# Moving a softmax's normalisation from the probabilities to the attention output

## Chip, cores and metric

One core of a Trainium2 chip runs the whole kernel. The metric is the device time of one execution, in microseconds.

## What is computed

Two sequences of 1024 tokens, 128 features, go through half a feed-forward layer (attention and experts), a sparse attention, and half a feed-forward layer again. The change lies in the sparse attention. Cut to what matters (B = 2 sequences; the program cuts 1024 tokens into tiles of 128; 8 heads):

```
x = x + 0.5 * ffn(layernorm(x))
x = x + attn(layernorm(x))
x = x + 0.5 * ffn(layernorm(x))

def attn(x):                                   # for every token t and head h
    c_kv = x @ W_dkv                           # 32 latent features per token
    I    = index scores of t against all earlier tokens
    idx  = top_k(I with the last 64 tokens set to +inf, 96)   # 64 local keys + 32 selected
    scores = (q_c . key_c[idx] + q_r . key_r[idx]) * scale
    attn   = softmax(scores)                   # over the 96 keys
    out    = sum_k attn[k] * value[idx[k]]     # value = c_kv @ W_uv
    return out @ W_out
```

W_uk, W_uv and W_out are folded by the kernel into two small matrices, so that keys and values of a token are both 32 latent features (plus 32 + 32 for the rotated part of the key).

## The kernel before

The attention runs over NB = 128 blocks of 16 tokens. A block has 16 x 8 = 128 rows (token, head), so scores and probabilities fill the 128 partitions; their 256 columns are 128 local positions and 4 x 32 selected ones. Blocks come in pairs, far, near, far, near (`place`). A far block lies in the second half of its sequence: its selected rows are fetched by POOL, four indirect DMAs (L620), into one of six buffers G. A near block lies in the first half: POOL makes one-hot matrices from the index list (L639, one to four per block), and PE multiplies the tables TAB by them (L1001). Sixteen blocks are a phase; there are 8. The selection for phase q (top 32 by `max`, `max_index`, `match_replace`, `dve_select`) runs on DVE in the steps of the phase before. The last piece of it, the near list, is made in iteration 16q - 3 of the loop (L1662 or L1664); SP stores it to DRAM and reads it back to all partitions (L501, L507); then POOL can make the phase's one-hots. The far list goes by PE and ACT (L1242) to POOL. 

A row of keys and values has ROWG = 128 columns: 64 of the rotated key, 32 latent (DC), and 32 that hold 1.0 (L598, `KVS[:, :, ROWKV:]`). Before the change the loop reads the first ROWKV = 96 only.

Every engine works in the order of its program, iteration i = 0 to 127:

- PE: `pe_turned(i)` (transposes the probabilities PB into bank 6, L1029; for near blocks the values too, L1032), `pe_keys(i+3)` (L995, L1001), `pe_scored(i+2)` (L1014, L1017, mask L1020), index scores L982 where due, `pe_mixed(i)` (values times probabilities into bank 7, L1045, L1048).
- DVE: `dve_inverse(i+1)` (L1697), `dve_keys(i+3)` (L1683, multiplies the keys by the rotation), `dve_least(i+2)` (L1692, the row minimum, since scores are held negated), every fourth iteration `dve_attended` (L1707, copies four blocks of bank 7 to OA), and the selection steps.
- ACT: `act_turned(i)` (L1271, bank 6 to PTS), the queries L1261, `act_scaled(i+1)` (L1284, multiplies the probabilities by 1/sum), `act_exp(i+2)` (L1278, exp with the row sum in `total` by `accum_out`), index scores L1249, L1252.
- SP moves OA to OAX (L515, 16 transfers a phase) after `oa_ready`; PE's last product (L951) needs all of them.

So the probabilities are normalised before they are transposed: exp and its sum on ACT, the reciprocal of one column on DVE, the scaling on ACT (`pn_ready`), then PE. Bank 7 holds four groups of 4 blocks, 32 partitions each.

Of the kernel before, what the change touches and what calls it, by code (L numbers as in the profile page):

```python
# [12 lines left out]
ALU = mybir.AluOpType  # L13
# [3 lines left out]
P = 128  # L17
# [179 lines left out]
def build(nc, ins, const_ap, rot_ap, mask_ap, out):  # L197
# [9 lines left out]
    with ExitStack() as ctx:  # L207
# [55 lines left out]
        total = sb("total", [P, 3])  # L263
        inverse = sb("inverse", [P, 3])
# [62 lines left out]
        KV64 = view("sel", (NT, DC))  # L327
# [24 lines left out]
        PTS = [ATTf[:, i * 3 * P:(i + 1) * 3 * P] for i in range(2)]  # L352
        PB = [ATTf[:, 6 * P + i * 2 * P:6 * P + (i + 1) * 2 * P] for i in range(3)]
# [53 lines left out]
        inverse_ready, pn_ready = sem("inverse_ready"), sem("pn_ready")  # L407
# [109 lines left out]
        def sp_sel(sp):  # L517
# [14 lines left out]
            for b in range(B):  # L532
                t = b * TB
                sp.dma_start(KV64[0:LW, t + 1:t + TB, :], KVS[LW:P, t:t + TB - 1, 2 * DR:ROWKV]).then_inc(kv64_loaded, 16)
                sp.dma_start(KV64[LW:P, t:t + TB, :], KVS[0:LW, t:t + TB, 2 * DR:ROWKV]).then_inc(kv64_loaded, 16)
                sp.dma_start(KV64[0:LW, t, :], KVS[0:LW, t, 2 * DR:ROWKV]).then_inc(kv64_loaded, 16)
# [448 lines left out]
        def pe_keys(pe, x):  # L985
# [5 lines left out]
            if far:  # L991
                d = 8 * q + k
                pe.wait_ge(gathered[d % GR], 16 * GB * (d // GR + 1))
                for g in range(GB):
                    m = pe.transpose(o[0:ROWKV, g * P:(g + 1) * P], G[d % GR][:, g, 0:ROWKV], ident)  # L995
            else:
                b, n = tile // TB, chunks(tile, k)
                for c in range(n):
                    pe.wait_ge(oh_ready, OH_AT[x][c] + 1)
                    for part in range(2):  # L1000
                        m = pe.matmul(o[0:ROWKV, :], TAB[part][:, 4 * b + c, 0:ROWKV], OH[OH_AT[x][c] % OHR][:, :],  # L1001
                                      start=(c == 0 and part == 0), stop=(c == n - 1 and part == 1))
# [19 lines left out]
        def pe_turned(pe, x):  # L1022

            q, far, tile, k = place(x)
            pe.wait_ge(pn_ready, x + 1)
            if x >= 1:
                pe.wait_ge(pts_ready, x)
            for part in range(2):
                m = pe.transpose(bank[6][:, part * P:(part + 1) * P], PB[x % 3][:, part * P:(part + 1) * P], ident)  # L1029
            if not far:  # L1030
                for g in range(GB):
                    m = pe.transpose(bank[6][:, 2 * P + g * DC:2 * P + (g + 1) * DC],  # L1032
                                     GTS[x % 3][2 * DR:ROWKV, g * P:(g + 1) * P], ident[2 * DR:ROWKV, 2 * DR:ROWKV])
            m.then_inc(tp_done, 1)

        def pe_mixed(pe, x):
# [4 lines left out]
            if slot == 0 and j >= 4:  # L1041
                pe.wait_ge(oa_ready, j - 3)
            o = bank[7][j % 4 * DC:(j % 4 + 1) * DC, slot * P:(slot + 1) * P]
            pts = PTS[x % 2]
            pe.matmul(o, KVS[:, tile, 2 * DR:ROWKV] if k >= 4 else KV64[:, tile, :], pts[:, 0:P], start=True, stop=True)  # L1045
# [756 lines left out]
```

## Time and profile before

| | |
|---|---|
| median of 3 runs | 2058.41 us (2049.06 to 2064.82) |
| the profiled execution | 2058.41 us |
| its span | 2056.6 us |
| attention loop (first L1278 to last L1707) | about 792 to 1432 us |
| busy in the whole span | PE 84%, DVE 63%, ACT 54%, POOL 27% |

A row of "lines" or of the page gives line, engine, operation, tiles (written <- read), shapes and count, then busy time and mean ns, then the engine's idle time before them and what ended it. A row of the order of time gives start, duration, engine and line; in brackets stands how long the engine was idle before it and which instruction ended that. PEld is the loading of weights, beside PE.

### The profile page before, as it was taken

Reading aid. Unit: us, or ns where it says so; the run is one execution under the profiler, and the core shown is the slowest. Engines: PE = TensorE matmul, PEld = TensorE weight load, DVE = VectorE, ACT = ScalarE, POOL = GpSimd, SP = SyncE. Lnnn points to the kernel's source line nnn. Section 1 sums busy time; section 2 is a strip of 40 time slices with the busy share of each in tenths; the row PEclk is TensorE's granted clock in tenths of the full one; section 3 lists DMA queues with packets and bytes.
Section 4 is the critical chain, followed back from the end, with each engine's and each line's share of the span. In section 5 each row is a group of like instructions: output and inputs, shape, how many; then the busy total and the mean of one; then the engine's idle time right before and its main releaser. Section 6 shows DMA issues by size and latency. Waiting matters only on the chain.

```text
span 2056.6 us, 33763 instructions
## 1 busy us (share of the span) xinstructions
PE 1720.3 (84%) x10588; PEld 999.4 (49%) x10588; DVE 1287.6 (63%) x3053; ACT 1111.6 (54%) x2328; POOL 548.3 (27%) x479
## 2 busy tenths in 40 slices
PE   3799999699967357888987978989489999969995
PEld 1344444477754114454654545556234444447774
DVE  5677775577785665464555645533467777557777
ACT  3367777388845343434344334323237767738883
POOL 6000000000001504786656867662500000000000
PEclk9699999699987566777567768567769999969998
DMA  4111110012102142101021111120211111002110
GB/s 132 64 49 50 48 46 9 27 66 83 51 2 88 62 110 49 42 28 50 28 63 46 29 46 31 43 64 18 92 62 49 50 50 44 9 30 85 61 52 21
DMA packets 66504, 104.26 MB, mean 51 GB/s; under 512 B 19432, under 2 KB 37296, under 8 KB 63280
## 3 DMA queue, kind: packets, MB, share of 16 engines
q1 hardware_dynamic: 56720, 84.86, 12.8%
q0 software_dynamic: 8192, 16.79, 2.8%
q8 instruction: 72, 1.18, 0.2%
q10 hardware_dynamic: 1456, 0.90, 0.2%
q14 instruction: 64, 0.52, 0.1%
HBM read 74.80 MB, written 8.59 MB: 41 GB/s over the span
## 4 chain that ended last, share of the span: by engine, by line
PE 58%; POOL 13%; issue 10%; DVE 8%; ACT 4%; SPq 3%; DVEq 2%; DMA 1%; ACTq 0%; another core or an unknown queue 0%; POOLq 0%
PE bank L701 10%; PE bank L847 8%; PE bank L685 7%; POOL onehot L639 7%; POOL arena L620 6%; PE bank L660 6%; PE bank L837 6%; PE bank L1001 2%; PE bank L1014 2%; ACT experts L1146 1%; PE bank L662 1%; PE bank L687 1%; PE bank L1029 1%; DVE arena L1313 1%; PE bank L1017 1%
## 5 line engine op out<-in xcount | busy, mean ns | idle before, releaser
L1313 DVE TENSOR_REDUCE arena<-bank 128x1 f32<-128x512 f32 (+3 forms) x768 | 382.9, 551 | 170.1 <-PE bank L662 117.3
L1073 ACT ACTIVATE arena<-bank 128x512 f32<-128x512 f32 (+3 forms) x768 | 335.2, 493 | 144.3 <-PE bank L687 121.5
L566 POOL TENSOR_TENSOR rstd<-vareps,neghalf 128x8 f32<-128x8 f32 x14 | 23.8, 1698 | 1168.0 <-DVE vareps L1306 1168.0
L660 PE MATMUL bank<-arena 72*128 72x512 bf16 (+3 forms) x768 | 259.8, 346 | 39.1 <-DMA arena<-arena 37.0
L620 POOL DMA_INDIRECT arena<-kv_rows,IDX x256 | 250.8, 980 | 155.9 <-ACT IDX L1242 86.7
L685 PE MATMUL bank<-arena 99*128 99x512 bf16 (+3 forms) x768 | 254.4, 335 | 6.0 <-ACT arena L1079 4.3
L639 POOL TENSOR_SCALAR onehot<-XT,const 128x512 fp32r<-128x512 f16 x136 | 212.4, 1573 | 160.7 <-DMA XT<-idx_rows 76.7
L701 PE MATMUL bank<-arena 128*32 128x512 f32 (+3 forms) x1536 | 225.4, 501 | 0.0
L1683 DVE TENSOR_TENSOR HN<-bank,RT 96x512 f32<-96x512 f32 x128 | 87.3, 682 | 206.8 <-PE bank L1001 144.2
L1371 DVE TENSOR_TENSOR experts<-arena,experts 128x512 fp32r<-128x512 f32 x256 | 171.6, 689 | 71.1 <-ACT experts L1146 71.1
L1144 ACT ACTIVATE arena<-bank,bias 128x512 f32<-128x512 f32 x256 | 185.6, 725 | 46.1 <-PE bank L837 46.0
L1278 ACT ACTIVATE ATT<-bank,col 128x256 f32<-128x256 f32 x128 | 60.6, 473 | 272.1 <-DVE col L1692 242.1
L837 PE MATMUL bank<-experts,experts 128*128 128x512 f32 x768 | 196.6, 403 | 7.5 <-ACT experts L1146 5.5
L1146 ACT ACTIVATE experts<-bank,bias 128x512 fp32r<-128x512 f32 x256 | 186.9, 730 | 0.0
L1001 PE MATMUL bank<-onehot,tab 128*96 128x512 f32 x272 | 123.8, 576 | 72.2 <-POOL onehot L639 72.2
L847 PE MATMUL bank<-experts,experts 128*128 128x512 f32 x768 | 182.3, 390 | 0.0
L685 PEld LDWEIGHTS bank<-arena 99*128 99x128 bf16 x768 | 75.4, 98 | 204.0 <-ACT arena L1073 139.9
L837 PEld LDWEIGHTS bank<-experts,experts 128*128 128x128 f32 x768 | 143.7, 192 | 54.5 <-ACT experts L1146 22.3
L847 PEld LDWEIGHTS bank<-experts,experts 128*128 128x128 f32 x768 | 144.2, 188 | 30.5
L660 PEld LDWEIGHTS bank<-arena 72*128 72x128 bf16 x768 | 77.7, 101 | 110.3 <-DVE arena L1313 44.9
L662 PE MATMUL bank<-mask_qk_b,ident_b 128*128 128x128 bf16 x512 | 117.3, 230 | 0.0
L687 PE MATMUL bank<-mask_kq_b,ident_b 128*128 128x128 bf16 x512 | 113.0, 222 | 0.0
(247 smaller groups left out, 2592.0 us busy)
## 6 DMA issues: line engine op xcount, KB each, us to landing
arena<-wt_rows SPq DMA_DIRECT2D x16, 1024.0 KB, 4.7
arena<-q_rows SPq DMA_DIRECT2D x192, 48.0 KB
arena<-k_rows SPq DMA_DIRECT2D x192, 48.0 KB
arena<-in_L_ffn_w SPq DMA_DIRECT2D x32, 256.0 KB, 5.1
arena<-arena SPq DMA_DIRECT2D x32, 256.0 KB
XT<-idx_rows SPq DMA_DIRECT2D x8, 1024.0 KB, 4.7
arena<-kv_rows,IDX POOLq DMA_INDIRECT x256
arena<-HN SPq DMA_DIRECT2D x32, 128.0 KB, 2.4
```

Source lines behind the costliest of these rows:

```text
L620: pool.indirect_dma_start(G[d % GR][:, g, :], None, kv_rows, bass.IndirectOffsetOnAxis(ap=IDX[:, q, k * GB + g:k * GB + g + 1], axis=0))\
L639: pool.tensor_scalar(OH[n % OHR][:, :], IDXB[:, k * BANK:(k + 1) * BANK], cst("key")[:, c:c + 1], None, ALU.is_equal)\
L660: m = pe.matmul(o[:, 0:hi - lo], QB[buf][s][0:ROWS, qt * P:(qt + 1) * P], KB[buf][s][0:ROWS, lo:hi], start=True, stop=True)
L685: m = pe.matmul(o[:, 0:hi - lo], KB[buf][s][0:rows, kc * P:(kc + 1) * P], QB[buf][s][0:rows, lo:hi], start=True, stop=True)
L701: m = pe.matmul(bank[6][r:r + STRIP, lo - hf * BANK:BANK], VS[buf][:, s, kc, :], PT[w % PT_RING][:, 0:(hf + 1) * BANK - lo], start=(kc == ...
L837: m = pe.matmul(bank[f][:, :], W1R[buf][w][:, f * P:(f + 1) * P], XR[x][:, tb * BANK:(tb + 1) * BANK], start=((w, x) == pairs[0]), stop=(( ...
L847: m = pe.matmul(bank[4 + k][:, :], W2R[buf][w][:, f, :], H1R[k][x][:, f, :], start=(f == 0 and (w, x) == pairs[0]), stop=(f == FC - 1 and ...
L1073: act.activation(PT[w % PT_RING][:, 0:m], bank[S_RING + w % S_RING][:, 0:m], ACT.Exp, scale=float(HD) ** -0.5)\
L1144: act.activation(H1[tb % 2][:, f, :], bank[f][:, :], ACT.Gelu_apprx_tanh, bias=bias1[buf][:, f:f + 1])
L1146: act.activation(H1R[tb % 2][0][:, f, :], bank[f][:, :], ACT.Gelu_apprx_tanh, bias=bias1[buf][:, f:f + 1]).then_inc(gelu_done, 1)
L1313: dve.tensor_reduce(rowmax[:, hf, s, qt:qt + 1], bank[u % S_RING][:, 0:n], AX_X, ALU.max).then_inc(max_done, 1)
L1371: dve.tensor_tensor(H1R[tb % 2][1][:, f, :], H1[tb % 2][:, f, :], H1R[tb % 2][0][:, f, :].bitcast(F32), ALU.subtract)\
```

## The change

The probabilities stay unnormalised. Keys and values are carried with their 32 columns of 1.0 (128 columns instead of 96, values 64 instead of 32), so `pe_mixed` yields in 64 partitions of bank 7 the weighted values and, in the 32 below them, the sum of the probabilities. `dve_attended` takes the reciprocal of these sums, 32 partitions x 512 columns, and multiplies. `act_scaled`, `dve_inverse`, `total`, `inverse` and the row sum of `act_exp` go; PE waits for `pb_ready` instead of `pn_ready`. PB has two buffers instead of three, bank 7 two groups instead of four (`oa_ready`, j - 1), the copy `act_turned` of a near block takes 512 columns instead of 384.

```diff
@@ build
-        KV64 = view("sel", (NT, DC))
+        KV64 = view("sel", (NT, 2 * DC))
+        RS = HNf[:, 3 * BANK:]
-        PTS = [ATTf[:, i * 3 * P:(i + 1) * 3 * P] for i in range(2)]
-        PB = [ATTf[:, 6 * P + i * 2 * P:6 * P + (i + 1) * 2 * P] for i in range(3)]
+        PTS = [ATTf[:, i * BANK:(i + 1) * BANK] for i in range(2)]
+        PB = [ATTf[:, 2 * BANK + i * 2 * P:2 * BANK + (i + 1) * 2 * P] for i in range(2)]
@@ sp_sel (three transfers per sequence)
-                sp.dma_start(KV64[0:LW, t, :], KVS[0:LW, t, 2 * DR:ROWKV]).then_inc(kv64_loaded, 16)
+                sp.dma_start(KV64[0:LW, t, :], KVS[0:LW, t, 2 * DR:]).then_inc(kv64_loaded, 16)
@@ pe_keys
-                    m = pe.transpose(o[0:ROWKV, g * P:(g + 1) * P], G[d % GR][:, g, 0:ROWKV], ident)
+                    m = pe.transpose(o[:, g * P:(g + 1) * P], G[d % GR][:, g, :], ident)
-                        m = pe.matmul(o[0:ROWKV, :], TAB[part][:, 4 * b + c, 0:ROWKV], OH[OH_AT[x][c] % OHR][:, :],
+                        m = pe.matmul(o[:, :], TAB[part][:, 4 * b + c, :], OH[OH_AT[x][c] % OHR][:, :],
@@ pe_turned
-            pe.wait_ge(pn_ready, x + 1)
+            pe.wait_ge(pb_ready, x + 1)
-                    m = pe.transpose(bank[6][:, 2 * P + g * DC:2 * P + (g + 1) * DC],
-                                     GTS[x % 3][2 * DR:ROWKV, g * P:(g + 1) * P], ident[2 * DR:ROWKV, 2 * DR:ROWKV])
+                    m = pe.transpose(bank[6][:, 2 * P + g * 2 * DC:2 * P + (g + 1) * 2 * DC],
+                                     GTS[x % 3][2 * DR:, g * P:(g + 1) * P], ident[2 * DR:, 2 * DR:])
@@ pe_mixed
-            if slot == 0 and j >= 4:
-                pe.wait_ge(oa_ready, j - 3)
-            o = bank[7][j % 4 * DC:(j % 4 + 1) * DC, slot * P:(slot + 1) * P]
+            if slot == 0 and j >= 2:
+                pe.wait_ge(oa_ready, j - 1)
+            o = bank[7][(j % 2) * 2 * DC:(j % 2 + 1) * 2 * DC, slot * P:(slot + 1) * P]
-            pe.matmul(o, KVS[:, tile, 2 * DR:ROWKV] if k >= 4 else KV64[:, tile, :], pts[:, 0:P], start=True, stop=True)
+            pe.matmul(o, KVS[:, tile, 2 * DR:] if k >= 4 else KV64[:, tile, :], pts[:, 0:P], start=True, stop=True)
-                rows = G[(8 * q + k) % GR][:, g, 2 * DR:ROWKV] if far else pts[:, 2 * P + g * DC:2 * P + (g + 1) * DC]
+                rows = G[(8 * q + k) % GR][:, g, 2 * DR:] if far else pts[:, 2 * P + g * 2 * DC:2 * P + (g + 1) * 2 * DC]
@@ act_sel, act_turned, act_exp
-            act_scaled(act, 0)
-                if i + 1 < NB:
-                    act_scaled(act, i + 1)
-            n = 2 * P if far else 3 * P
+            n = 2 * P if far else BANK
-            if x >= 3:
-                act.wait_ge(tp_done, x - 2)
-            act.activation(PB[x % 3], bank[2 + x % 2][:, 0:2 * P], ACT.Exp, scale=-1.0, bias=col[:, x % 3:x % 3 + 1],
-                           accum_out=total[:, x % 3:x % 3 + 1]).then_inc(pb_ready, 1)
-
-        def act_scaled(act, x):
-
-            act.wait_ge(inverse_ready, x + 1)
-            act.activation(PB[x % 3], PB[x % 3], ACT.Identity, scale=inverse[:, x % 3:x % 3 + 1]).then_inc(pn_ready, 1)
+            if x >= 2:
+                act.wait_ge(tp_done, x - 1)
+            act.activation(PB[x % 2], bank[2 + x % 2][:, 0:2 * P], ACT.Exp, scale=-1.0, bias=col[:, x % 3:x % 3 + 1]).then_inc(pb_ready, 1)
@@ dve_sel, dve_keys
-            dve_inverse(dve, 0)
-                if i + 1 < NB:
-                    dve_inverse(dve, i + 1)
-            dve.tensor_tensor(GTS[x % 3][0:ROWKV].rearrange("p (t j) -> p t j", j=NSEL),
-                              bank[4 + x % 2][0:ROWKV, :].rearrange("p (t j) -> p t j", j=NSEL),
-                              RT[0:ROWKV, :].unsqueeze(1).broadcast_to([ROWKV, BT, NSEL]), ALU.mult).then_inc(gts_ready, 1)
+            dve.tensor_tensor(GTS[x % 3].rearrange("p (t j) -> p t j", j=NSEL), bank[4 + x % 2][:, :].rearrange("p (t j) -> p t j", j=NSEL),
+                              RT[:, :].unsqueeze(1).broadcast_to([P, BT, NSEL]), ALU.mult).then_inc(gts_ready, 1)
@@ dve_inverse, dve_attended
-        def dve_inverse(dve, x):
-
-            dve.wait_ge(pb_ready, x + 1)
-            dve.reciprocal(inverse[:, x % 3:x % 3 + 1], total[:, x % 3:x % 3 + 1]).then_inc(inverse_ready, 1)
-
-            o = bank[7][j % 4 * DC:(j % 4 + 1) * DC, :]
+            r = (j % 2) * 2 * DC
+            o, inv = bank[7][r:r + DC, :], RS[r:r + DC, :]
+            dve.reciprocal(inv, bank[7][r + DC:r + 2 * DC, :])
+            dve.drain()
-                m = dve.tensor_copy(OA[:, :, t0:t0 + 2 * BT].rearrange("p h (g t) -> p g h t", t=4),
-                                    o[:, cols].rearrange("p (g h t) -> p g h t", h=NH, t=4))
+                m = dve.tensor_tensor(OA[:, :, t0:t0 + 2 * BT].rearrange("p h (g t) -> p g h t", t=4),
+                                      o[:, cols].rearrange("p (g h t) -> p g h t", h=NH, t=4),
+                                      inv[:, cols].rearrange("p (g h t) -> p g h t", h=NH, t=4), ALU.mult)
```

## Rows read from the trace of the kernel before

**Rows 1.** The page's busy line, and busy time by stretches for one stretch.

```profile
PE 1720.3 (84%) x10588; PEld 999.4 (49%) x10588; DVE 1287.6 (63%) x3053; ACT 1111.6 (54%) x2328; POOL 548.3 (27%) x479
...
core 0: us, PE busy (x) PEld busy (x) DVE busy (x) ACT busy (x) POOL busy (x), PEclk, DMA share, GB/s
943.00:1025.00 82.00, 76.97 (x478) 46.08 (x479) 44.30 (x106) 32.08 (x88) 52.33 (x47) 0.56 0.13 42
```

**Rows 2.** Waits, 784 to 1434 us (total, times, longest), and who L1029 waited for.

```profile
POOL onehot L639 <- DMA XT<-idx_rows: 76.7, 7, 15.1
POOL arena L620 <- ACT IDX L1242: 30.5, 4, 9.9
...
  ACT ATT L1284: 9.7, 20
```

**Rows 3.** Chain that ended last: shares from 861 to 943 us, then single pieces.

```profile
by line: POOL onehot L639 37.7%; POOL arena L620 31.0%; issue 23.4%; PE bank L1001 3.7%; PE bank L995 2.1%; PE bank L1014 0.5%; PE bank L1029 0.4%; PE bank L1017 0.4%; PE bank L1045 0.4%; PE bank L1048 0.3%; PE bank L1020 0.3%; POOLq L638 0
...
793.44 0.40 ACT ATT L1284
...
1077.70 0.41 ACT ATT L1284
...
966.23 0.72 PE bank L1014 x2
...
1000.09 0.72 PE bank L1014 x2
```

**Rows 4.** Groups by line and shape: removed operations, ACT's copy, reciprocals, one product.

```profile
L1284 ACT ACTIVATE ATT<-ATT,inverse 128x256 f32<-128x256 f32 x128 | 64.4, 503 | 38.1 <-DVE inverse L1697 30.8 <-issue 6.9
L1278 ACT ACTIVATION_READ_ACCUMULATOR ATT<-bank,col 128x1 f32 x128 | 24.7, 193 | 0.0
L1271 ACT ACTIVATE ATT<-bank 128x384 f32<-128x384 f32 x64 | 31.1, 486 | 36.1 <-PE bank L1032 26.4 <-remote 6.4 <-issue 3.3
L1697 DVE RECIPROCAL inverse<-total 128x1 f32<-128x1 f32 x128 | 19.2, 150 | 11.9 <-ACT ATT L1278 10.0 <-issue 1.9
L1338 DVE RECIPROCAL arena<-bank 128x8 f32<-128x8 f32 x64 | 8.7, 177 | 39.6 <-PE bank L710 39.6
L1451 DVE RECIPROCAL g<-g 128x16 f32<-128x16 f32 x2 | 0.5, 252 | 0.1
L1460 DVE TENSOR_TENSOR g<-top 128x16 f32<-128x16 f32 x2 | 0.3, 166 | 0.0
```

**Rows 5.** PE at the low clock: order of time at 972 us, groups from 966 to 1003.

```profile
972.32 0.64 PE L1048 MATMUL bank<-ATT,arena 128*32 128x32 f32 x8
973.50 0.63 PE L1032 MATMUL bank<-const,HN 32*128 32x32 f32 x4
...
L1048 PE MATMUL bank<-ATT 128*32 128x32 f32 x32 | 2.5, 244 | 0.0
L1032 PE MATMUL bank<-const,HN 32*128 32x32 f32 x16 | 2.5, 295 | 0.0
```

**Rows 6.** Order of time on DVE at two phase ends, first and last of seven.

```profile
863.00 0.76 DVE L1707 COPY arena<-bank 32x256 f32<-32x256 f32 x2
866.93 0.69 DVE L1683 TENSOR_TENSOR HN<-bank,RT 96x512 f32<-96x512 f32 x1 [2.45 <-PE bank L995]
867.91 0.42 DVE L1692 TENSOR_REDUCE col<-bank 128x1 f32<-128x256 f32 x1 [0.30 <-PE bank L1020]
868.43 0.18 DVE L1664 CAST bidh<-bidx 128x32 f16<-128x32 uint32 x1
...
1357.74 0.69 DVE L1683 TENSOR_TENSOR HN<-bank,RT 96x512 f32<-96x512 f32 x1 [1.20 <-PE bank L995]
1358.98 0.42 DVE L1692 TENSOR_REDUCE col<-bank 128x1 f32<-128x256 f32 x1 [0.55 <-PE bank L1020]
```

**Rows 7.** Order of time, one of the 22 further places.

```profile
968.36 0.77 DVE L1707 COPY arena<-bank 32x256 f32<-32x256 f32 x2
972.14 0.69 DVE L1683 TENSOR_TENSOR HN<-bank,RT 96x512 f32<-96x512 f32 x1
975.81 0.65 PE L1017 MATMUL bank<-HN,ATT 96*32 96x128 f32 x8
```

**Rows 8.** Order of time at the end of the attention loop.

```profile
1431.26 0.77 DVE L1707 COPY arena<-bank 32x256 f32<-32x256 f32 x2 [3.71 <-PE bank L1048]
```

More of the change, by code:

```diff
@@ L262, in build @@
         col = sb("col", [P, 3])
-        total = sb("total", [P, 3])
-        inverse = sb("inverse", [P, 3])
         best = sb("best", [P, NSEL])
@@ L406, in build @@
         gt_done, gts_ready, s_done, min_ready, pb_ready = (sem(n) for n in ("gt_done", "gts_ready", "s_done", "min_ready", "pb_ready"))
-        inverse_ready, pn_ready = sem("inverse_ready"), sem("pn_ready")
         tp_done, pts_ready, ob_done, oa_ready = (sem(n) for n in ("tp_done", "pts_ready", "ob_done", "oa_ready"))
@@ L533, in sp_sel @@
                 t = b * TB
-                sp.dma_start(KV64[0:LW, t + 1:t + TB, :], KVS[LW:P, t:t + TB - 1, 2 * DR:ROWKV]).then_inc(kv64_loaded, 16)
-                sp.dma_start(KV64[LW:P, t:t + TB, :], KVS[0:LW, t:t + TB, 2 * DR:ROWKV]).then_inc(kv64_loaded, 16)
-                sp.dma_start(KV64[0:LW, t, :], KVS[0:LW, t, 2 * DR:ROWKV]).then_inc(kv64_loaded, 16)
+                sp.dma_start(KV64[0:LW, t + 1:t + TB, :], KVS[LW:P, t:t + TB - 1, 2 * DR:]).then_inc(kv64_loaded, 16)
+                sp.dma_start(KV64[LW:P, t:t + TB, :], KVS[0:LW, t:t + TB, 2 * DR:]).then_inc(kv64_loaded, 16)
+                sp.dma_start(KV64[0:LW, t, :], KVS[0:LW, t, 2 * DR:]).then_inc(kv64_loaded, 16)
             sp_near(sp, 0)
@@ L1028, in pe_turned @@
             for part in range(2):
-                m = pe.transpose(bank[6][:, part * P:(part + 1) * P], PB[x % 3][:, part * P:(part + 1) * P], ident)
+                m = pe.transpose(bank[6][:, part * P:(part + 1) * P], PB[x % 2][:, part * P:(part + 1) * P], ident)
             if not far:
                 for g in range(GB):
-                    m = pe.transpose(bank[6][:, 2 * P + g * DC:2 * P + (g + 1) * DC],
-                                     GTS[x % 3][2 * DR:ROWKV, g * P:(g + 1) * P], ident[2 * DR:ROWKV, 2 * DR:ROWKV])
+                    m = pe.transpose(bank[6][:, 2 * P + g * 2 * DC:2 * P + (g + 1) * 2 * DC],
+                                     GTS[x % 3][2 * DR:, g * P:(g + 1) * P], ident[2 * DR:, 2 * DR:])
             m.then_inc(tp_done, 1)
```

## Prediction

> **What bounds the kernel now.** I read the busy line of the page, then the busy time by stretches [rows 1]: the change touches only the attention loop, from about 784 to 1432 us, and there no engine is full. PE, DVE and POOL take turns. The waits [rows 2] say who is last: POOL waits 76.7 us in seven places for the list of near indices (XT, L507) and 30.5 us for the far ones, while PE and its weight loads wait for ACT's scaling at L1029 only 9.7 us, in 20 places. The chain [rows 3] says the same: from 861 to 943 us it is POOL's one-hots and gathers; the "issue" part (23.4%) is mostly POOL standing before the index list. In the stretch 943 to 1025 the chain is PE's own instructions in unbroken order, at a granted clock of 0.56. So work taken off ACT is worth next to nothing, work added on DVE is worth what DVE cannot hide.
>
> **Step 1, removed.** Per block (128 of them): the scaling on ACT, 503 ns, the accumulator read that belongs to `accum_out`, 193 ns, and DVE's 150 ns reciprocal of one column [rows 4]. That is 64.4 + 24.7 us of ACT and 19.2 us of DVE. In the chain through the whole loop L1284 stands twice, 0.4 us each [rows 3]; I count -0.8 us. If all of PE's waits for it were on the path, it would be 9.7 us [rows 2].
>
> **Step 2, PE.** Keys, tables and transposes become 128 or 64 columns wide where they were 96 or 32, but the moving side, which sets the matmul, stays, except that L1032 moves 64 columns. L1048 now loads 64 columns of weights for 32 moving ones. Rows at the low clock [rows 5]: eight L1048 take 0.64 us and one 0.244, so they start (0.64 - 0.244)/7 = 0.057 us apart; four L1032, which load 128 columns for 32 moving ones, start (0.63 - 0.295)/3 = 0.112 us apart. Half of 0.112 is 0.056: 64 columns of load just fit under the present spacing, and L1032 with 64 moving columns stays set by its load. I take 0. Upper bound: L1048 as slow as L1032, 8 x 0.055 = 0.44 us, on the 50 places where it is on the chain, 22 us. ACT's copy in near blocks grows from 384 to 512 columns: at most a third of its 486 ns [rows 4], nearer 0.1 us; it is three times on the chain: +0.3 us. The six KV64 transfers double their bytes; they are issued at about 652 to 658 us by the trace and first needed after 780: nothing. The two-bank rings (PB, bank 7) add no wait: `act_exp(i+2)` follows `act_turned(i)`, which has already waited for the same transposes, and `oa_ready` is asked for four blocks after its DVE work.
>
> **Step 3, DVE: the dear part.** `dve_attended` (32 times) gets a reciprocal of 32x512 from PSUM, a drain, and two products in place of two copies. Products: two 256-column copies take 0.76 us [rows 6], and I give the product the same. The reciprocal is not in the trace at this width. The nearest rows [rows 4]: 128x1 150 ns, 128x8 177 ns, 128x16 252 ns, against 166 ns for a product of 128x16. So a reciprocal does not run at one element per 1.07 ns as (166 - 150)/15 would have it. Line through 1 and 16: 6.8 ns an element, 0.252 + 496 x 0.0068 = 3.6 us. Line through 8 and 16: 9.4 ns, 4.9 us. The short ones may hide part of their work in the fixed time, which flattens the first line, and the second rests on two rows with different sources; I take 4.3 us, between them. Lower bound, from a plain 512-column row (L1683): 0.69 us [rows 6]. DVE adds 32 x 4.3 = 138 us to its 1287.6 and loses 19.2 [rows 1, 4].
>
> The Trainium skill ("VectorE: DVE Perf Modes", "First, the fixed hardware budget") says that `Reciprocal` runs iterative-divide operations with a repeat count of 8; with the 0.96 GHz of its "Specifications" an estimate from it is 512 x 8 / 0.96 = 4.3 us for one. By that rule the trace agrees from 16 elements on (252 ns against 166), and the change would add what step 3 adds; a reader who believed one element per cycle would find it free.
>
> In its iteration DVE gains 4.3 + 0.07 (drain) - 0.14 = 4.23 us, between `dve_least(i+2)` and the select steps, and `dve_keys(i+4)` queues behind it. What DVE idles there is given back. Three kinds of place:
>
> (a) *Seven phase ends.* The near index list is made in iteration 16q-3, one after an `attended`; POOL waits for it. In [rows 6] the copies start at 863.00, DVE then idles 2.45 us before the keys and 0.30 before the least, and the list's cast comes at 868.43; SP's two transfers and POOL follow it. New delay 4.23 - 2.75 = 1.5 us. The smallest idles are 1.1 us (around 1030 us) and the last place's 1.20 + 0.55 = 1.75; over all seven they add to 15.4, so 7 x 4.23 - 15.4 = **14.2 us**. All of it reaches POOL, which waits 76.7/7 = 11 us on average there.
>
> (b) *22 further places.* PE's second L1017 behind the copies needs the keys behind them. In [rows 7] copies start at 968.36, keys at 972.14, PE reads at 975.81: 972.14 + 4.23 + 0.69 - 975.81 = 1.25 us late. Done for each of the 22, the positive ones add to 34.4 us (from -0.7 to 3.6 each). Six lie in the two stretches whose chain is POOL nearly throughout (861 to 943, 1186 to 1267) and are hidden: 12.7 us. Of the 10.6 us in the two stretches that are half POOL's (780 to 861, 1105 to 1186) I take half, the remaining 11.0 us whole: **16.3 us**. Bounds 0 and 34.4.
>
> (c) *The end.* The place at 1414 us stalls PE 1.7 us. The one at 1424.84 delays the last least by 4.23 less 0.66 of idle; PE's transposes can take up 1.5 of that: 2.1. The last `attended` [rows 8] has nothing beside it, SP's 16 transfers wait: 4.4. Together **8.2 us**.
>
> **Sum:** 14.2 + 16.3 + 8.2 - 0.8 + 0.3 = +38.2 us. The profiled run has a span of 2056.6 and a time of 2058.41, which is also the median: 2058.4 + 38.2 = **2096.6 us** (+1.9%).
>
> **Rivals.**
> - *Interior all hidden* (POOL and the low-clock PE absorb (b)): 14.2 + 8.2 - 0.5 = +21.9, 2080 us. For it: POOL idles at the phase ends whatever comes before. Against: the chain between 965 and 1001 us is PE alone.
> - *Nothing hidden:* 14.2 + 34.4 + 8.2 - 0.5 = +56.3, 2115 us. For it: POOL's one-hots wait for PE too (L639 for L1001).
> - *The reciprocal is cheap* (0.69 us as the plain 512-column rows): 0.69 + 0.07 - 0.14 = 0.6 us is under the idle at every phase end and every positive stall of (b) goes but for a few tenths; the tail +0.8, less 0.5: 2059 us. It decides below about 1.7 us for one reciprocal. Against: the 252 ns row.
> - *Faster:* with a cheap reciprocal, PE without its waits for ACT keeps the full clock. Place: 965 to 1003 and 1297 to 1335 us, where PE alone is the chain: 966.23 to 1000.09 [rows 3], 33.9 us at the low clock (1.2 GHz), half of it at 2.4. Twice 17 is 34 us less, 2024 us. Against: PE hardly waits for ACT there, so nothing changes for it.
> - *The wider weight loads show:* +22 us on top of the sum, 2119 us. Against: the spacing of L1032.
>
> **Chances.** The sum, with 2085 to 2110 for its own range: 0.57. Interior hidden 0.15, nothing hidden 0.12, cheap reciprocal 0.09, faster 0.03, wider loads 0.04. The range 2070 to 2120 leaves out the cheap reciprocal and the faster case. One per cent, about what a measurement of this kernel can tell from no change, is 2079 us: interior hidden is split between same and slower. Faster 0.04, same 0.16, slower 0.80.
>
> **What would show it.** Reciprocals 32x512, 32 of them, near 4.3 us (138 us of DVE; DVE busy about 1287.6 + 138 - 19 = 1407 us, ACT about 1111.6 - 89 + 7 = 1029 us). POOL's wait for XT near 76.7 + 14 us. PE's L1017 held by DVE's keys after each `attended`. A span of eight L1048 at the low clock still 0.64 us. The prediction is wrong if the reciprocal takes under 2 us, if the granted clock in 965 to 1003 us changes its level, or if POOL's wait for XT does not grow.

## The result and the profile after

The changed kernel takes 2115.59 us (median of four runs, 2113.15 to 2126.50) against 2054.39 us for the kernel before on the same chips (four runs, 2049.06 to 2064.82). The ratio is 1.0331, with a 95% interval of 1.0291 to 1.0370: between 60 and 76 us slower. The forecast had the sign right and the size wrong: +1.9%, with a range that ends at +3.0%. Ratios and their intervals leave out a run that is more than 1.5% above the fastest of its kernel: one of four of the kernel with the wide work alone (2127.70 us) and one of 19 of the kernel before (2070.95 us). The profiled execution of the kernel after took 2128.8 us, its span is 2127.0 us.

The busy line of the page of the kernel after, to be read against the first line of [rows 1]:

```profile
PE 1800.0 (85%) x10588; PEld 1085.1 (51%) x10588; DVE 1378.9 (65%) x2957; ACT 1050.6 (49%) x2072; POOL 549.1 (26%) x479
```

DVE has 91 us more, which is about what the reciprocals add less the short ones; ACT has 61 us less. But PE, whose instruction count is the same, has 80 us more, and its weight loads 86 us more. The forecast gave PE nothing. The groups by line and shape in the attention loop (784 to 1505 us):

```profile
L1684 DVE RECIPROCAL HN<-bank 32x512 f32<-32x512 f32 x32 | 107.4, 3356 | 7.9 <-PE bank L1046 7.0
...
L1690 DVE TENSOR_TENSOR arena<-bank,HN 32x256 f32<-32x256 f32 x64 | 24.1, 411 | 3.1 <-issue 0.9
...
L1266 ACT ACTIVATE ATT<-bank 128x512 f32<-128x512 f32 x64 | 37.9, 593 | 44.9 <-PE bank L1030 37.5 <-issue 5.6 <-remote 1.6
...
L1046 PEld LDWEIGHTS bank<-ATT 128*64 128x64 f32 x512 | 61.6, 205 | 0.0
...
L1046 PE MATMUL bank<-ATT 128*64 128x32 f32 x512 | 58.0, 272 | 0.0
```

The reciprocal takes 3.36 us, not 4.3. ACT's copy is 0.11 us longer than in [rows 4], as said. L1046 is L1048 of before, with 64 columns of weights. Its span in the order of time on PE, at the low clock, with L1030 (L1032 of before), which now moves 64 columns:

```profile
976.12 1.01 PE L1046 MATMUL bank<-ATT,arena 128*64 128x32 f32 x8
...
977.68 0.69 PE L1030 MATMUL bank<-const,HN 64*128 64x64 f32 x4
```

The eight took 0.64 us in [rows 5] and take 1.01 us here; L1030 went from 0.63 to 0.69. In the chain, where overlaps are cut away, the same eight are one piece. Its pieces in order of time (start, us, what), first a whole block of the kernel before, then of the kernel after:

```profile
972.53 0.43 PE bank L1048 x8
972.96 0.62 PE bank L1029 x2
973.58 0.56 PE bank L1032 x4
974.14 1.02 PE bank L995 x4
975.15 0.72 PE bank L1014 x2
975.88 0.58 PE bank L1017 x8
976.46 0.33 PE bank L1020
976.79 0.57 PE bank L1045 x2
```

```profile
976.33 0.80 PE bank L1046 x8
977.13 0.62 PE bank L1027 x2
977.75 0.62 PE bank L1030 x4
978.37 1.04 PE bank L993 x4
979.41 0.72 PE bank L1012 x2
980.13 0.58 PE bank L1015 x8
980.72 0.33 PE bank L1018
981.04 0.62 PE bank L1043 x2
```

So one costs 0.43/8 = 0.054 us with 32 columns of load and 0.80/8 = 0.100 us with 64. The block takes 4.8 us before (0.43 + 0.62 + 0.56 + 1.02 + 0.72 + 0.58 + 0.33 + 0.57) and 5.3 us after, and 0.37 of that 0.5 is L1046. The shares of the chain by line in the attention loop, of before (784 to 1432 us) and of after (784 to 1503 us):

```profile
by line: POOL onehot L639 22.3%; issue 20.0%; POOL arena L620 19.3%; PE bank L1001 7.1%; PE bank L1014 5.2%; PE bank L1029 4.3%; PE bank L1017 4.2%; PE bank L1045 3.9%; PE bank L995 3.8%; PE bank L1048 2.9%; PE bank L1020 2.4%; PE bank L103
```

```profile
by line: issue 20.0%; POOL onehot L637 15.2%; POOL arena L618 11.0%; PE bank L999 9.4%; PE bank L1046 6.8%; PE bank L1012 6.0%; PE bank L1027 5.3%; PE bank L1043 5.3%; PE bank L1015 4.9%; PE bank L993 3.9%; PE bank L1030 3.1%; PE bank L1018
```

The loop is 71 us longer. POOL's two lines fall from 41.6% of 648 us (270 us) to 26.2% of 719 us (188 us). PE's lines grow, L1048/L1046 from 19 to 49 us most of all, and the others too: the tables (L1001/L999) from 46 to 68 us, the transposes (L1029/L1027) from 28 to 38 us. DVE is not among the twelve lines that the view shows, but it is in the chain: its pieces add to 29 us of the kernel after against 4 us before. 10.2 us of that are three steps through the drain behind the reciprocal (L1685), and 3.4 us are the last reciprocal, at 1499 us. The kernel after is held more by PE than the one before was, and a little more by DVE.

The waits from 784 to 1500 us (total, times, longest):

```profile
POOL onehot L637 <- DMA XT<-idx_rows: 90.9, 7, 19.3
...
POOL arena L618 <- ACT IDX L1237: 45.0, 3, 18.6
...
POOL onehot L637 <- PE bank L999: 33.6, 8, 7.4
...
PE bank L1015 <- DVE HN L1669: 6.7, 6, 1.8
```

POOL's wait for the near list is 90.9 us, to a tenth what the forecast gave (76.7 + 14.2). The experiments show that the reciprocal is not the only thing behind it, and that it is cheaper than the forecast had it, so the agreement to a tenth is a coincidence. And PE waits for DVE's keys in six places for 6.7 us, where the forecast had 22 places and put 16.3 us of them on the path.

### The profile page after: what moved, and what is told of

Read it like the earlier page. It is cut to its first block, busy times and chain, and to the rows that moved or that the text cites. A ratio compares the mean times of both kernels' runs of the same rounds, so it can differ in the third digit from the quotient of the medians.

```text
span 2127.0 us, 33446 instructions
## 1 busy us (share of the span) xinstructions
PE 1800.0 (85%) x10588; PEld 1085.1 (51%) x10588; DVE 1378.9 (65%) x2957; ACT 1050.6 (49%) x2072; POOL 549.1 (26%) x479
## 4 chain that ended last, share of the span: by engine, by line
PE 61%; issue 10%; POOL 9%; DVE 8%; ACT 4%; DVEq 3%; SPq 2%; DMA 1%; ACTq 0%; POOLq 0%; another core or an unknown queue 0%
PE bank L699 10%; PE bank L845 8%; PE bank L683 7%; PE bank L658 6%; PE bank L835 5%; POOL onehot L637 5%; POOL arena L618 4%; PE bank L999 3%; PE bank L1046 2%; PE bank L1012 2%; PE bank L1027 2%; PE bank L1043 2%; PE bank L1015 2%; ACT experts L1144 2%; PE bank L660 1%
## 5 line engine op out<-in xcount | busy, mean ns | idle before, releaser
L637 POOL TENSOR_SCALAR onehot<-XT,const 128x512 fp32r<-128x512 f16 x136 | 212.7, 1575 | 196.5 <-DMA XT<-idx_rows 90.9
L1669 DVE TENSOR_TENSOR HN<-bank,RT 128x512 f32<-128x512 f32 x128 | 87.9, 687 | 207.1 <-PE bank L999 164.3
L999 PE MATMUL bank<-onehot,tab 128*128 128x512 f32 x272 | 129.0, 602 | 48.6 <-POOL onehot L637 48.4
```

The lines of the kernel that those rows point to most:

```text
L637: pool.tensor_scalar(OH[n % OHR][:, :], IDXB[:, k * BANK:(k + 1) * BANK], cst("key")[:, c:c + 1], None, ALU.is_equal)\
L999: m = pe.matmul(o[:, :], TAB[part][:, 4 * b + c, :], OH[OH_AT[x][c] % OHR][:, :], start=(c == 0 and part == 0), stop=(c == n - 1 and part ...
```

## The experiments

Three theories were to be told apart. By the first, the forecast's own, the time is DVE's: a burst of some 3.4 us, 32 times, makes keys and index lists late. By the second it is PE's: the 64-column weight loads. By the third it is the granted clock's: the change leaves PE at the low level in more of the blocks, and that costs more than either part alone. "Blocks at the low level" below are counted in the order of time on PE, by the span of the pair of 128x128 transposes of each block (L1029 before, L1027 after): 0.69 us at 1.2 GHz and 0.44 us at 2.4 GHz. Of the 128 blocks the kernel before has 63 at the low level, the kernel after 82. The expectations go by an earlier count of some 124 blocks, with 62 and 78. All ratios are against the kernel before on the same chip. "Points" are hundredths of that ratio, some 20.5 us each. An expectation often names two theories with the time that each would give: R, the reciprocal on DVE costs, and L, the wide loads on PE cost.

### The parts alone

**The kernel after, with the reciprocal replaced by a copy of the same shape.** The products then multiply by the sum instead of its inverse.

```diff
-            dve.reciprocal(inv, bank[7][r + DC:r + 2 * DC, :])
+            dve.tensor_copy(inv, bank[7][r + DC:r + 2 * DC, :])
```

> The changed kernel with the 32x512 reciprocal replaced by a copy of the same 32x512 (3.36 us becomes about 0.69 us, 32 times); this leaves out the division, the output is not normalised. Weight loads stay 64 columns wide. Theory R (the reciprocal on VectorE is what costs): the time falls by 45 us or more from 2116 us, to within 15 us of the kernel before (2054 to 2069 us). Theory L (the 64-column weight loads of the mixing matmuls, 8 a block, 1.01 instead of 0.64 us at the low clock, are what costs): it stays at 2095 us or above. Both in like parts: 2075 to 2090 us.

Measured: 2115.11 us, 1.0309 (1.0248 to 1.0371). The copy takes 0.69 us in place of 3.36, DVE's busy time falls by 81 us, and the time is that of the kernel after within the intervals. In the kernel as it was changed, the dear part of the forecast costs nothing that can be measured, as theory L had it. POOL's wait for the near list is 83.1 us without a single long reciprocal, so only 7.8 of the 90.9 us go with it.

```profile
POOL onehot L637 <- DMA XT<-idx_rows: 83.1, 7, 16.7
```

**The kernel before, plus the reciprocal.** It writes into an unused place; nothing else is changed.

```diff
             o = bank[7][j % 4 * DC:(j % 4 + 1) * DC, :]
+            dve.reciprocal(RS[j % 4 * DC:(j % 4 + 1) * DC, :], o)
+            dve.drain()
```

> The kernel before with one thing added: a reciprocal of 32x512 from bank 7 into spare space, and a drain, ahead of the copies of dve_attended; its result is not used. Theory R: 3.36 us more on DVE 32 times gives +45 us or more over the kernel before (2100 us or above). Theory L: under +20 us (below 2075 us). Both in like parts: +25 to +40 us.

Measured: 2131.73 us, 1.0435 (1.0390 to 1.0480), slower than the whole change, and as theory R had it: with only one of the two theories this run and the last don't go together. The order of time after one burst shows why:

```profile
977.15 3.36 DVE L1704 RECIPROCAL HN<-bank 32x512 f32<-32x512 f32 x1
...
984.20 0.14 DVE L1698 RECIPROCAL inverse<-total 128x1 f32<-128x1 f32 x1
...
984.38 0.51 ACT L1285 ACTIVATE ATT<-ATT,inverse 128x256 f32<-128x256 f32 x1 [5.68 <-DVE inverse L1698]
...
984.94 0.69 PE L1030 MATMUL bank<-const,ATT 128*128 128x128 f32 x2 [3.19 <-ACT ATT L1285]
```

The reciprocal of one column, which ACT's scaling needs, stands behind the burst; ACT waits 5.68 us, PE 3.19. In the loop the matmuls of this line wait 67.6 us in 32 places, against 3.5 us in five before (the 9.7 us in 20 places of [rows 2] count the weight loads' waits as well).

```profile
PE bank L1030 <- ACT ATT L1285: 67.6, 32, 4.2
```

**The wide PE work alone.** The kernel after with the scaling of the kernel before kept and `dve_attended` copying as before; the diff to the kernel before is the change's in `KV64`, `pe_keys`, `pe_turned`, `pe_mixed` and the two-deep rings. The core of it:

```diff
-            pe.matmul(o, KVS[:, tile, 2 * DR:ROWKV] if k >= 4 else KV64[:, tile, :], pts[:, 0:P], start=True, stop=True)
+            pe.matmul(o, KVS[:, tile, 2 * DR:] if k >= 4 else KV64[:, tile, :], pts[:, 0:P], start=True, stop=True)
```

> The changed kernel's wide TensorE work (128-column keys, 64-column values, two groups in bank 7, 512-column copies on ScalarE) with the scaling of the probabilities on ScalarE, the one-column reciprocal and the plain copies of the kernel before; the 32 sums in bank 7 are not used. Theory R: within 10 us of the kernel before. Theory L: +40 us or more. Both in like parts: +20 to +35 us.

Measured: 2103.74 us, the median of three runs that lie wide apart (2090.74 to 2117.63), 1.0252 (1.0191 to 1.0314), with 82 blocks at the low level. So the part that was costed at nothing gives, alone, some two and a half points.

**The scaling taken out, nothing else.** The output is not divided by the sum of the weights.

```diff
-            pe.wait_ge(pn_ready, x + 1)
+            pe.wait_ge(pb_ready, x + 1)
...
-                if i + 1 < NB:
-                    act_scaled(act, i + 1)
...
-                if i + 1 < NB:
-                    dve_inverse(dve, i + 1)
```

> The kernel before without the scaling of the probabilities (ScalarE 0.50 us, accumulator read 0.19 us, one-column reciprocal 0.15 us, each 128 times) and without anything in its place; it leaves out the normalisation. The prediction's step 1 says -0.8 us, that is no difference that can be measured, and at most -9.7 us. If the two hops from exp to the transposes mattered, 20 us or more would go.

Measured: 2045.01 us, 0.9982 (0.9952 to 1.0012): nothing, as step 1 said. ACT loses 67 us of work and the kernel does not notice.

**The same, plus the reciprocal.** This is the change without the wide PE work.

```diff
+            dve.reciprocal(RS[j % 4 * DC:(j % 4 + 1) * DC, :], o)
+            dve.drain()
```

> e_recip_only (kernel before plus a 32x512 reciprocal and drain in dve_attended, 2132 us against 2050) with the scaling of the probabilities, its accumulator read and the one-column reciprocal taken out; narrow weight loads as before; it leaves out the normalisation. In e_recip_only TensorE waited 67.6 us for the scaled probabilities, where it waited 3.5 us before. Theory H (the burst on DVE holds back the small reciprocal, so the scaling comes late, and that is most of the 82 us): 2070 to 2085 us. Theory B (the burst itself, through keys and index list, is what costs, whatever the scaling does): 2110 us or more. Set against the changed kernel (about +65 us) it also gives the price of the wide TensorE work when the reciprocal is there.

Measured: 2094.97 us, 1.0197 (1.0138 to 1.0255), between what the two theories gave. Against the kernel with no scaling and no burst the reciprocal costs 2.15 points, 44 us. And against the reciprocal with the scaling (1.0435) the removal of the scaling is worth 2.4 points, though it is worth nothing where DVE has no burst. And against the kernel after (1.0331) the wide PE work is worth 1.3 points, some 28 us, on top of the burst.

### What in the wide work costs

**The values' weight loads back to 32 columns.** The kernel after with the copy for the reciprocal, as above, and only `pe_mixed` narrow again: it leaves out the columns of ones. Tables, gathered rows, transposes, rings and transfers stay wide.

```diff
-            pe.matmul(o, KVS[:, tile, 2 * DR:] if k >= 4 else KV64[:, tile, :], pts[:, 0:P], start=True, stop=True)
+            pe.matmul(o, KVS[:, tile, 2 * DR:ROWKV] if k >= 4 else KV64[:, tile, 0:DC], pts[:, 0:P], start=True, stop=True)
...
-                rows = G[(8 * q + k) % GR][:, g, 2 * DR:] if far else pts[:, 2 * P + g * 2 * DC:2 * P + (g + 1) * 2 * DC]
+                rows = G[(8 * q + k) % GR][:, g, 2 * DR:ROWKV] if far else pts[:, 2 * P + g * 2 * DC:2 * P + g * 2 * DC + DC]
```

> e_copy_for_recip (changed kernel, copy in place of the reciprocal; 2115 us) with only the values' weight loads in pe_mixed taken back from 64 to 32 columns; keys, transposes and ScalarE's copies stay wide, the output is not normalised. Theory W (the 64-column loads of 8 matmuls a block, +0.37 us at the low clock and +0.19 at the full one, are the wide part's cost): 30 us or more go, to 2085 us or below. If the rest of the wide work costs it: 2105 us or above.

Measured: 2061.49 us, 1.0033 (1.0004 to 1.0062). The same two lines of the order of time as above, now of this kernel:

```profile
965.99 0.64 PE L1046 MATMUL bank<-ATT,arena 128*32 128x32 f32 x8
...
967.18 0.69 PE L1030 MATMUL bank<-const,HN 64*128 64x64 f32 x4
```

The span of the eight is back at 0.64 us and 2.76 of the 3.09 points of the copy kernel are gone, 54 us by the medians. What is left is 0.3 of a point (0.04 to 0.62) against the kernel before, and half a point against the kernel with the scaling taken out, 0.9982: the wide tables, transposes and transfers, the shorter rings, the drain and the short copy. The number of blocks at the low level is back at 63, from 83.

### Is it the place of the burst?

**`dve_attended` two iterations later,** away from the iteration before the near list's steps.

```diff
-                if i >= 1 and i % 4 == 0:
+                if i >= 6 and i % 4 == 2:
                     dve_attended(dve, i // 4 - 1)
```

> The changed kernel with dve_attended called two iterations later (iteration 4m+2), behind the iteration that makes the near index list instead of one ahead of it. The prediction's part (a), that the reciprocal delays the index list at seven phase ends: with 3.36 us instead of 4.3 it is 7 x 3.3 - 15.4 = 7.6 us, so 5 to 12 us should go (2104 to 2111 us). If the list's path did not matter: no change, or slower.

Measured: 2125.73 us, 1.0346 (1.0285 to 1.0407). POOL's wait for the near list falls from 90.9 to 85.9 us, that for the far one rises from 45.0 to 48.8, PE's 6.7 us of waits for DVE's keys at the second L1017 are gone, and the time does not move. The 5 to 12 us that were to go did not.

**The reciprocal and product in two halves of 256 columns,** in iterations 0 and 2 of four, both after the whole group.

```diff
-                if i >= 1 and i % 4 == 0:
-                    dve_attended(dve, i // 4 - 1)
+                if i >= 4 and i % 2 == 0:
+                    dve_attended(dve, i // 4 - 1, i % 4 // 2)
```

> The changed kernel with each reciprocal and its product done in two halves of 256 columns, the second two iterations after the first; all work is kept (64 reciprocals of about 1.7 us in place of 32 of 3.36). Theory P (a burst longer than what DVE idles at that place costs; halves fit in the idle time): 15 us or more below the changed kernel, about 2095 us. Theory L (the wide weight loads on TensorE and its clock are what holds the changed kernel up): within 8 us of it.

Measured: 2128.04 us, 1.0348 (1.0287 to 1.0410). Nothing is gained. With the wide loads in place neither where the burst stands nor how long it is in one piece matters.

### The granted clock

Idle bf16 matmuls ahead of the near blocks' tables keep PE at 2.4 GHz in more of the loop. They write a bank that the real matmul then starts afresh, so nothing of the result changes. The edit is the same in the five kernels that have it, four here and one in the next section:

```diff
                 b, n = tile // TB, chunks(tile, k)
+                for extra in range(20 if x % PER == 2 and q else 6):
+                    pe.matmul(o[:, :], ident_b[:, :], maskb[:, 0:2, :].rearrange("p v n -> p (v n)"), start=True, stop=True)
                 for c in range(n):
```

**In the kernel before.**

> The kernel before with idle matmuls added on TensorE: 6 of 128x128 by 128x512 (bf16) ahead of the key matmuls of every near block, 20 at the seven phase starts, where TensorE stands waiting for POOL's one-hots; they write into the bank that the key matmuls then overwrite. Before, 62 of 124 blocks seen ran at the low granted clock; every slowed kernel had 78 to 85. Theory C (the granted clock falls in TensorE's waits and stays low for blocks after them): fewer than 40 blocks at the low clock, and the time falls by 20 us or more. If the clock doesn't follow this: as many low blocks, and 10 to 80 us more for the added work.

Measured: 2025.14 us, 0.9853 (0.9820 to 0.9887), faster than both kernels. One stretch of the busy times by stretches, with the same columns as in [rows 1]:

```profile
943.00:1025.00 82.00, 76.26 (x628) 46.12 (x632) 49.42 (x118) 36.73 (x104) 53.45 (x48) 0.94 0.18 56
```

The group by line and shape of the idle matmuls (443 of the 482 are in the trace):

```profile
L999 PE MATMUL bank<-maskb,ident_b 128*128 128x512 bf16 x443 | 116.0, 404 | 7.0 <-issue 6.5 <-DVE HN L1685 0.4
```

The granted clock of that stretch is 0.94 where it was 0.56, and the DMA moves 56 GB/s where it moved 42. 116 us of idle matmuls are paid for: 23 blocks are at the low level instead of 63. What one block gains stands in the chain of this kernel, whose lines from here on are two above those of before:

```profile
982.26 0.44 PE bank L1031 x2
982.70 0.37 PE bank L1034 x4
983.07 0.57 PE bank L995 x4
983.64 0.41 PE bank L1016 x2
984.06 0.35 PE bank L1019 x8
984.41 0.22 PE bank L1022
984.63 0.34 PE bank L1047 x2
```

With 0.25 us for the eight products (a piece of the same chain at 974.58 us) that is 2.95 us at the high level, against 4.8 us at the low one in the block of the kernel before shown above.

**In the kernel after.**

> The changed kernel with the same idle matmuls. Theory C (some 30 us of the change's cost is that 16 more blocks run at the low clock): fewer than 50 blocks at the low clock, and the distance between this and e_busy_before is 30 to 45 us, against 65 us between the two without them. If the clock is no cause of the change's cost, the distance stays 60 us or more.

Measured: 2131.35 us, 1.0381 (1.0340 to 1.0422), no faster than the kernel after, with some 37 blocks at the low level instead of 82 and a mean granted clock of 0.861 instead of 0.801. The two kernels with idle matmuls lie 106 us apart, where the theory of the clock gave 30 to 45. That the low level is what makes the change dear falls with this run. What stands in its place, in the order of time around a burst:

```profile
1002.64 3.35 DVE L1686 RECIPROCAL HN<-bank 32x512 f32<-32x512 f32 x1
...
1005.68 0.60 PE L1048 MATMUL bank<-ATT,arena 128*64 128x32 f32 x8
...
1009.27 0.67 DVE L1671 TENSOR_TENSOR HN<-bank,RT 128x512 f32<-128x512 f32 x1
...
1010.00 0.43 PE L1017 MATMUL bank<-HN,ATT 96*32 96x128 f32 x8 [1.96 <-DVE HN L1671]
...
1012.63 1.01 PE L1048 MATMUL bank<-ATT 128*64 128x32 f32 x8
```

PE has the high level (the eight in 0.60 us; granted clock 1.00 from 1002 to 1010 us), stands 1.96 us before the keys that are late behind the reciprocal, and within half a microsecond of its return is at the low level (0.58 from 1010 to 1012.5 us; the next eight take 1.01 us). Here are the stalls of the forecast's place (b), 20.4 us in 16 places in the loop where the kernel after had 6.7 in six, and the drain behind the reciprocal (L1687) is in the chain with 6.1%, 44 us:

```profile
PE bank L1017 <- DVE HN L1671: 20.4, 16, 3.2
...
by line: issue 17.6%; PE bank L997 10.4%; POOL onehot L637 10.1%; POOL arena L618 8.2%; PE bank L1001 7.3%; DVEq L1687 6.1%; PE bank L1048 5.4%; PE bank L1045 4.4%; PE bank L1014 4.4%; PE bank L1029 4.3%; PE bank L1017 3.6%; DVEq L1619 3.6%
```

The time won by a faster PE is lost again waiting for DVE.

**In the kernel after with the copy for the reciprocal,** and **in the kernel with reciprocal and without scaling** (each leaves out what its twin above leaves out).

> e_copy_for_recip with the idle matmuls of e_busy_before (2025 us). With the clock held up, the wide work costs its full-clock price: 128 x (0.19 + some 0.06) = 32 us at most. Theory D (in e_busy_after DVE's reciprocal burst is the bound, which is why the higher clock gave it nothing): 2035 to 2060 us here, some 80 us less than e_busy_after. If TensorE's wide work is the bound there: 2100 us or above.

> e_recip_no_scaling (narrow, reciprocal, no scaling; 2095 us) with the idle matmuls. Theory D: the burst is the bound at the full clock, so it stays within 15 us of 2095 us or above. If the wide work bounds e_busy_after: 2050 us or below.

Measured: 2069.89 us, 1.0111 (1.0081 to 1.0140), with 30 blocks at the low level; and 2110.55 us, 1.0308 (1.0275 to 1.0341), with 32. The second is as theory D had it. The first missed: 10 us above its range, 61 us below the kernel after with idle matmuls instead of 80, and 45 us above the kernel before with them, where the full-clock price was put at 32 us at most. Together the ratios make a table:

| | without the idle matmuls | with them |
|---|---|---|
| neither burst nor wide loads | 0.9982 (0.9952 to 1.0012) | 0.9853 (0.9820 to 0.9887) |
| wide loads alone | 1.0309 (1.0248 to 1.0371) | 1.0111 (1.0081 to 1.0140) |
| burst alone | 1.0197 (1.0138 to 1.0255) | 1.0308 (1.0275 to 1.0341) |
| both | 1.0331 (1.0291 to 1.0370) | 1.0381 (1.0340 to 1.0422) |

(The first line is without scaling on the left and with it on the right; taking it out changed nothing on the left. The wide loads alone still have a copy of 0.69 us and a drain in place of the reciprocal.) On the left the wide loads cost 3.3 points and the burst 2.2, which would add to 5.4, and together they give 3.5: with the wide loads in, the burst adds 0.2 of a point, inside the intervals. On the right the burst costs 2.7 points on top of the wide loads and 4.6 without them, and the wide loads alone 2.6, so most of their price stays with the clock held up. How dear the burst is depends on whether PE or DVE is late first. A kernel with DVE's burst gains nothing from the idle matmuls, and the one with the burst alone loses 1.1 points by them, for which no run here gives the reason; one without it gains 1.3 to 2 points.

### The index list earlier

In every kernel here POOL waits between 55.8 and 92.7 us in the loop for the near list. In the kernel before, the index scores for the far list's first half were put two iterations earlier:

```diff
-            units += [(base - 5 + 2 * half + h // 2, 2 * q, half, h) for h in range(NIH)]
+            units += [(base - 7 + 4 * half + h // 2, 2 * q, half, h) for h in range(NIH)]
```

> The kernel before with one thing changed: the first four index-score matmuls of the next phase (L982, 2.08 us in iteration 16q-4, on TensorE's path to the near index list) issued in iterations 16q-7 and 16q-6 instead of 16q-5 and 16q-4. If TensorE's order in front of the index list sets POOL's wait, 1 to 2 us go at each of six phase ends: 6 to 12 us less than the kernel before. If something else does: no difference.

Measured: 2039.63 us, 0.9939 (0.9902 to 0.9975). POOL's waits fall from 76.7 to 63.2 us (near) and from 30.5 to 23.0 us (far) against [rows 2].

> Both things that helped the kernel before: the four index-score matmuls two iterations earlier (2040 us) and the idle matmuls (2025 us). If they act on different things (TensorE's order ahead of the index list; the granted clock) the gains add: about 2010 us. If the earlier index scores only helped by way of the clock: about 2025 us.

Measured, with the idle matmuls as well: 2050.58 us, 0.9991 (0.9955 to 1.0028). The two gains do not add, together they are none. The wait for the near list is 59.3 us, that for the far one 30.4, where the idle matmuls alone had 55.8 and 17.5. Why the far list is later in the combination was not found. The fastest version is the kernel before with idle matmuls alone.

## Why the prediction was wrong, point by point

**What bounds the kernel:** right for the kernel before, and held for too long. The reading was that work added on DVE is worth what DVE cannot hide. PE's chain from 965 to 1001 us was seen, and the rival "wider weight loads" was named, but a place where PE is alone on the chain is just where an added PE cost shows in full.

**Step 1, the scaling:** right. -0.8 us was said, and the measured ratio of 0.9982 (0.9952 to 1.0012) agrees with it. What it did not say is that the hop's price depends on DVE: with the burst in front of `dve_inverse` it is 2.4 points. The change needs its removal, since the reciprocal alone with the hop kept is slower (1.0435) than the whole change.

**Step 2, the weight loads: this is the step that failed.** It took 0 for L1048 because four L1032 of 128 columns start 0.112 us apart and half of that fits under 0.057. But L1032 is a transpose, L1048 a product; the pace was carried from one to the other. For the product 64 columns cost 0.100 us each, not 0.056: 0.37 us more in a block at the low level and 0.80/8 against 0.43/8 says that the cost goes almost with the columns. The bound that was kept, 0.44 us a block, was right for a block. Multiplied by the 50 places where L1048 stood on the chain of the kernel before it gave 22 us and, as a rival, 2119 us (+2.9%), near the +3.3% measured; 22 us is also near the 1.3 points (28 us) that the wide work costs on top of the burst, which is about the whole miss of the forecast. (The rival "nothing hidden", 2115 us, is as near in number and wrong in what it says: of its 34.4 us of waits for late keys 6.7 came.) The 50 places were still too few. Once the loads were slower, more places were PE's: 66 pieces, 49 us against 19, and without the burst the wide work costs 3.3 points. An estimate from the rows, for the kernel with the copy: 83 blocks at the low level by 0.37 us are 31 us, the 45 others by 0.19 us (0.44 against 0.25 us, both in chains at the high level) are 9 us, so 40 of the 54 us that the narrow loads gave back. Whether the rest goes with the 20 further blocks at the low level (83 against 63), each of which costs up to 1.9 us more than at the high one (4.8 us against 2.95 by the pieces of the chain), is not shown. The pair with idle matmuls speaks against that as the whole of it: 30 and 23 blocks at the low level, by the same estimate 30 us for the loads, and 45 us between the medians. The chance of 0.04 for this rival was far too small for a cost that no row showed for that kind of instruction.

The Trainium skill ("TensorE: Matmul & The Clock Gate", "LDWEIGHTS (loading the stationary operand)") states that a weight load takes its number of columns divided by 1.2, in nanoseconds, whatever the rows. An estimate from it is 27 ns for 32 columns and 53 for 64. The traces come near it at the high level, with 0.25/8 = 31 ns and 0.44/8 = 55 ns for one product, and show nearly twice the estimates at the low level, 54 and 100 ns. At the low level this estimate would have fitted under the spacing of 57 ns and backed the zero; against the 31 ns of the high level, which step 2 did not look at, it would have spoken against it.

**Step 3, the reciprocal:** the mechanism was right, the price was too high, and the effect of a microsecond was too low. It takes 3.36 us: (3356 - 150)/511 = 6.3 ns an element, nearer the line through 1 and 16 elements (3.6 us) than the one through 8 and 16 (4.9 us). The estimate from the Trainium skill's page ("VectorE: DVE Perf Modes"), 4.3 us, is 28% above the measured. With 3.36 us DVE gains 3.3 us an iteration, not 4.23, and the forecast's own sums shrink: (a) 7 x 3.3 - 15.4 = 7.7 us, (b) 14 us at most, (c) 8.2 - 3 x 0.93 = 5.4 us, 27 us at most. For (b) each of the 22 places is done again with DVE's idle just before the keys given back, which the 34.4 us of the forecast did not do (with 4.23 us it is 29 us). Measured without the wide loads: 44 us. The sum moved fixed times against each other and left the clock as it was; with the burst 83 blocks are at the low level, without it 61. That this makes up the difference is not shown.

**(a)** The phase ends: no gain from moving the burst away from them (1.0346). POOL's wait for the near list tells more, one trace a kernel. Without scaling it is 69.7 us with neither part, 83.1 with the wide loads, 85.7 with the burst, 90.9 with both. So each part alone adds 13 to 16 us, and the burst on top of the wide loads 7.8, about the 7.7 us of the sum above. The delay of the list by the burst is there; on the path it is hidden as far as the slower PE makes the list late anyway. That the 14.2 us of the forecast agree with the growth from 76.7 to 90.9 is chance.

**(b)** The keys behind the burst: 6.7 us in six places in the kernel after, 11.6 us in 13 with narrow loads and no scaling, 20.4 us in 16 where PE is held at the high level. The mechanism is there, and hidden as far as PE itself is late: moved two iterations on, the burst leaves none of these waits, and the time stays.

**(c)** The end of the loop was not tried by itself. The chain of the kernel after has the last reciprocal in it with its full 3.36 us.

**The sum:** 38.2 us was forecast, all but half a microsecond of it DVE's, and 60 to 76 us came. How much is whose depends on the order in which the parts are taken: the burst is worth 0.2 of a point on top of the wide loads and 2.2 alone, the wide loads 1.3 and 3.3. In the kernel after, the forecast's mechanism is hidden. That the sign came out right is no merit of it there, since either part alone makes the kernel slower. That +1.9% is also what the burst alone costs (1.0197) is luck too: the forecast had the reciprocal too dear and the price of each microsecond too low. The conditions named for being wrong were the reciprocal under 2 us, another clock level in 965 to 1003 us and an unchanged wait for XT; none came true. The sign that told, "eight L1048 at the low clock still 0.64 us" (1.01 us came), stood in the list of what to look at and was the first row to read.

## What to carry to other kernels

Take the pace of a weight load from the same kind of instruction, at both levels of the clock: a transpose's spacing need not be a product's. Where a change makes an engine slower that is second on the path, price it over all its instructions and not over those on the present chain, for the chain moves to it. And try parts of a change both alone and on top of each other: here they cost 3.3 and 2.2 points alone and 3.5 together, and a hop worth nothing became worth 2.4 points as soon as something long stood ahead of it in its queue.

## What the runs showed of the hardware

A product with f32 operands, 32 moving columns and 64 columns of weights takes 0.100 us in a row of eight at 1.2 GHz and 0.055 us at 2.4 GHz, against 0.054 and 0.031 us with 32 columns: with the same moving side, its time goes almost with the columns of weights. A DVE reciprocal of f32 from PSUM takes 3.36 us for 512 elements in a partition where a copy takes 0.69 us. In the stretch from 943 to 1025 us of the kernel before PE is busy for 77 of 82 us with small f32 products and has a granted clock of 0.56; 116 us of idle bf16 matmuls spread over the loop lift the stretch to 0.94 and make the whole kernel 1.5% faster, though they are work for nothing.
